# Moving the first norm's inverse root from VectorE to GpSimd in a graph network kernel, with a pipeline one slot shorter and a new end

## The reference

```python
h = x @ W_loop.T ;  g = h @ Wg_loop.T
vals = (h + b_loop) * sigmoid(g + bg_loop)
x1 = layernorm(x + relu((adj.T == 1) @ vals))        # first norm, eps 1e-5
msg = (adj == 1) @ x1
out = layernorm(x1 + msg @ weight[0] + bias)         # second norm
```

## Time and profile before

| | us |
|---|---|
| median of 3 runs | 167.06 (166.71 to 167.41) |
| profiled execution: its own time | 167.7 |
| profiled execution: span from first to last instruction | 166.0 |
| PE busy | 153.1 (92%) |
| DVE busy | 145.5 (88%) |
| ACT busy | 126.2 (76%) |
| POOL busy | 79.9 (48%) |
| message copy on ACT, L534, mean of 31 | 0.580 |
| first norm on ACT for one graph, L582, one instruction | 0.483 |
| second norm on ACT for one graph, L551, mean of 112 | 0.392 |
| memset of one column on POOL, L964 | 0.098 |

### The profile page before, as it was taken

One profiled execution on the slowest core, in us unless ns is written; L12 is line 12 of the kernel. 1 busy time (PEld: TensorE's weight loads), 2 busy tenths in 40 slices (PEclk: granted clock), 3 DMA queues, 4 the chain that ended last, 5 costly groups with the idle time before them and its releaser, 6 DMA issues.

```text
span 166.0 us, 3902 instructions
## 1 busy us (share of the span) xinstructions
PE 153.1 (92%) x1068; PEld 141.9 (85%) x1068; DVE 145.5 (88%) x583; ACT 126.2 (76%) x287; POOL 79.9 (48%) x194
## 2 busy tenths in 40 slices
PE   6499899999999999999999999999999999998910
PEld 2278789999999999999999999999999999997910
DVE  1425999999999999999999999999999999999770
ACT  3318767679988888888888888899888887754670
POOL 4070456264737474747466464646374544446000
PEclk9999999999999999999999999999999999999996
DMA  4999999989598979798998979797979261131133
GB/s 123 332 300 315 396 399 396 391 281 321 153 300 288 380 222 348 275 310 308 285 348 245 374 224 381 211 371 206 370 243 360 31 226 39 41 117 63 67 124 139
DMA packets 18857, 42.76 MB, mean 258 GB/s; under 512 B 2112, under 2 KB 2368, under 8 KB 18832
## 3 DMA queue, kind: packets, MB, share of 16 engines
q1 hardware_dynamic: 13968, 25.24, 42.3%
q0 software_dynamic: 4720, 17.11, 33.8%
q10 hardware_dynamic: 144, 0.13, 0.2%
HBM read 34.08 MB, written 8.39 MB: 256 GB/s over the span
## 4 chain that ended last, share of the span: by engine, by line
PE 85%; DVE 5%; issue 3%; DMA 3%; ACT 1%; ACTq 0%; DVEq 0%; POOLq 0%
PE hg_ps L381 33%; PE msg_ps L411 16%; PE loop_ps L393 15%; PE y_ps L432 15%; DMA gate_b<-gate_bias_dram 3%; PE hg_ps L432 2%; PE hg_ps L428 2%; DVE s_sb L735 1%; ACT gate L524 1%; PE y_ps L428 1%; PE hg_ps L411 1%; ACT out_sb L551 1%; DVE stats L742 0%; DVE hg_ps L638 0%; DVE z_sb L753 0%
## 5 line engine op out<-in xcount | busy, mean ns | idle before, releaser
L381 PE MATMUL hg_ps<-w_all,xt_sb 128*128 128x256 f32 x256 | 63.3, 393 | 2.2 <-DVE w_all L641 2.2
L333 POOL TENSOR_SCALAR x<-s_sb,rstd,nmr 128x128 f32<-128x128 f32 x125 | 55.0, 452 | 3.5 <-issue 0.2
L381 PEld LDWEIGHTS hg_ps<-w_all,xt_sb 128*128 128x128 f32 x256 | 48.2, 198 | 8.9 <-DVE w_all L641 3.1
L515 ACT ACTIVATE hg_ps<-gate_b 128x1024 f32<-128x1024 f32 (+1 forms) x32 | 32.0, 1002 | 9.6 <-DVE vals L727 6.0
L551 ACT ACTIVATE out_sb<-z_sb,rstd 128x128 f32<-128x128 f32 x112 | 38.0, 392 | 0.3 <-DVE rstd L691 0.2
L325 POOL TENSOR_TENSOR nmr<-mean_neg,rstd 128x4 f32<-128x4 f32 x31 | 6.2, 201 | 63.6 <-DVE rstd L691 63.6
L393 PEld LDWEIGHTS loop_ps<-vals,adj_sb 128*128 128x128 f32 x256 | 33.3, 192 | 2.7 <-issue 1.3
L393 PE MATMUL loop_ps<-vals,adj_sb 128*128 128x128 f32 x256 | 33.9, 275 | 0.5 <-DVE s_sb L735 0.5
L411 PE MATMUL msg_ps<-adjt_sb,x 128*128 128x128 f32 x248 | 33.0, 276 | 0.0
L524 ACT ACTIVATE gate<-hg_ps 128x512 f32<-128x512 f32 x32 | 19.1, 596 | 17.0 <-PE hg_ps L381 16.8
L432 PE MATMUL y_ps<-w,msg_t 128*128 128x128 f32 x232 | 30.7, 275 | 0.0
(11 more groups left out here) (66 smaller groups left out, 103.8 us busy)
## 6 DMA issues: line engine op xcount, KB each, us to landing
xt_sb<-x_t_dram SPq DMA_DIRECT2D x32, 256.0 KB, 6.3
x_sb<-x_dram SPq DMA_DIRECT2D x32, 256.0 KB, 6.4
adj_sb<-adj_dram POOLq DMA_DIRECT2D x16, 512.0 KB, 4.5
adjt_sb<-adj_t_dram POOLq DMA_DIRECT2D x16, 512.0 KB, 6.7
out<-out_sb SPq DMA_DIRECT2D x32, 256.0 KB, 3.9
const_sb<-consts_dram POOLq DMA_DIRECT2D x1, 192.0 KB, 5.0
w_all<-w_loop_both_dram ACTq DMA_DIRECT2D x1, 128.0 KB, 2.3
gate_b<-gate_bias_dram POOLq DMA_DIRECT2D x1, 128.0 KB, 4.9
```

What stands on the lines that cost most here:

```text
L333: last = nc.gpsimd.tensor_scalar(x1[:, q % X1_RING, batch(b)], s_sb[:, q % S_RING, batch(b)], r[:, b:b + 1], n[:, b:b + 1], ALU.mult, ALU.add)
L381: last = nc.tensor.matmul(hg_ps[:, q % 2, b, :], xt_sb[:, q % XT_RING, batch(b)], w_gate, start=False, stop=True, skip_group_check=True)
L515: nc.scalar.activation(hg_ps[:, q % 2, 0:graphs, :], gate_b[:, None, :].broadcast_to([P, graphs, 2 * P]), ACT.Copy).then_inc(seeded, 1)
```

## The change

Five things change.

1. DVE no longer computes the first norm's inverse root. It computes var + eps and the negated mean of four columns (`first_moments`) behind the first norm's statistics. POOL raises the variance to the power -0.5 with one elementwise instruction against a constant tile `power`, waits for it, multiplies, and writes x1 as before.
2. The lags become LOOP 1, NORM1 1, MSG 2, Y 3, Z 4, STAT2 5, NORM2 6 (before 1, 2, 3, 4, 5, 6, 7).
3. DVE's nine-step chain serves the second norm alone, 4 columns wide, with one step behind each large instruction.
4. POOL issues the load of `adj` in odd slots and that of `adj_t` in even slots, where it issued both in odd slots.
5. The end is new: `LAST` is 27; only groups 29 and 30 (`INJECTED`) get x1 by the identity matmul, groups 28 and 31 by a DVE add; norm1 of groups 30 and 31 (`SHARED`) is split between ACT and POOL or ACT and DVE; the last chains serve the groups 27 to 29 and 30 to 31; POOL does the second norm of group 27 and of a quarter of group 31; the store of group 30 is issued by ACT.

```diff
-LOOP_LAG, NORM1_LAG, MSG_LAG, Y_LAG, Z_LAG, STAT2_LAG, NORM2_LAG = 1, 2, 3, 4, 5, 6, 7
-LAST = GROUPS - 4
+LOOP_LAG, NORM1_LAG, MSG_LAG, Y_LAG, Z_LAG, STAT2_LAG, NORM2_LAG = 1, 1, 2, 3, 4, 5, 6
+LAST = GROUPS - 5
+CHAIN_A, CHAIN_B = (LAST, LAST + 1, LAST + 2), (LAST + 3, LAST + 4)
+INJECTED = (LAST + 2, LAST + 3)
+SHARED = (GROUPS - 2, GROUPS - 1)
...
             def norm1(q):
                 if exists(q):
-                    t = q + NORM1_LAG
-                    pool.wait_ge(chain_done[t % 2], chain_end(t))
-                    r, n = rstd[:, t % RSTD_RING, 0, :], nmr[:, t % 2, :]
+                    r, n = rstd1[:, q % 2, :], nmr[:, q % 2, :]
+                    pool.wait_ge(mean_done, 2 * q + 2)
+
+                    nc.gpsimd.tensor_tensor(r, var1[:, q % 2, :], power[:, :], ALU.pow).then_inc(rstd1_done, 1)
+                    pool.wait_ge(rstd1_done, q + 1)
+                    nc.gpsimd.tensor_tensor(n, mean_neg[:, q % 2, :], r, ALU.mult).then_inc(nmr_done, 1)
...
+            nc.gpsimd.memset(power[:, :], -0.5).then_inc(power_ready, 1)
             pool.dma_start(gate_b[:, :], gate_bias).then_inc(bias_in, 16)
...
                 norm1(t - NORM1_LAG)
                 if t % 2 == 1:
                     load_adj(t // 2 + 3)
+                else:
                     load_adjt(t // 2 + 2)
...
             loop_sum(GROUPS - 1)
-            message_weights(GROUPS - 4)
-            messages(GROUPS - 3)
+            inject(GROUPS - 3)
             message_weights(GROUPS - 3)
             messages(GROUPS - 2)
+            inject(GROUPS - 2)
+            messages(GROUPS - 1)
             message_weights(GROUPS - 2)
...
-            messages(GROUPS - 1)
             message_weights(GROUPS - 1)
...
-            copy_messages(GROUPS - 4)
-            norm2(GROUPS - 7, every)
             copy_messages(GROUPS - 3)
-            norm2(GROUPS - 6, every)
+            norm2(LAST - 1, every)
+            shared_norm1(GROUPS - 2)
+            shared_norm1(GROUPS - 1)
             copy_messages(GROUPS - 2)
...
+            norm2(LAST + 3, every)
+            act.wait_ge(out_done, LAST + 3)
+            act.dma_start(out[LAST + 3], out_sb[:, (LAST + 3) % OUT_RING, :])\
+                .then_inc(out_st[(LAST + 3) % OUT_RING], 16)
...
+            def first_moments(q):
+
+                m = stats[:, q % STATS_RING, 0:2, :].rearrange("p c (i k) -> p (c i) k", k=3)
+                dve.wait_ge(bn1_done, q + 1)
+
+                await_count(dve, nmr_done, q - 1)
+                ts(var1[:, q % 2, :], m[:, :, 2], 1.0 / P, EPS, ALU.mult, ALU.add).then_inc(mean_done, 1)
+                yield
+                ts(mean_neg[:, q % 2, :], m[:, :, 1], -1.0, None, ALU.mult).then_inc(mean_done, 1)
...
+            last_second_sum(LAST + 1)
+            first_sum(GROUPS - 1)
+            first_stats(GROUPS - 1, 0)
+            first_stats(GROUPS - 1, 1)
+            odd_steps = find_odd()
+            next(odd_steps)
+            for _ in first_moments(GROUPS - 1):
+                pass
+            next(odd_steps, None)
+            last_second_stats(LAST + 1, 0)
+            last_second_stats(LAST + 1, 1)
+            last_second_stats(LAST + 2, 0)
+            last_second_stats(LAST + 2, 1)
+            last_norm1(GROUPS - 1)
+            for _ in last_chain(0, CHAIN_A):
                 pass
+            last_second_stats(LAST + 3, 0)
+            last_second_stats(LAST + 3, 1)
             dve.wait_ge(odd_count, 1)
             nc.vector.tensor_copy(flag[:, :], aux_ps[0:1, 2 * P:2 * P + 1]).then_inc(flag_ready, 1)
+            last_second_sum(LAST + 4)
+            last_second_stats(LAST + 4, 0)
+            last_second_stats(LAST + 4, 1)
+            for _ in last_chain(1, CHAIN_B):
                 pass
+            last_norm2(LAST + 4, (0, 1, 2))
```

More of the change, by code:

```diff
@@ L336, in norm1 @@
-                    last.then_inc(x1_done, 1)
+                        await_count(pool, msg_done, q - X1_RING + 1)
+                        await_count(pool, z_done, q - X1_RING + 1)
+                        for b in range(2 if q in SHARED else GB):
+                            done = nc.gpsimd.tensor_scalar(
+                                x1[:, q % X1_RING, batch(b)], s_sb[:, q % S_RING, batch(b)],
+                                r[:, b:b + 1], n[:, b:b + 1], ALU.mult, ALU.add)
+                        done.then_inc(x1_done, 1)
@@ L413, in messages, with inject @@
                     last.then_inc(msg_done, 1)
+            def inject(q):
+                pe.wait_ge(consts_in, 16)
+                await_x1(q)
+                pe.wait_ge(vals_done, GROUPS - 1)
+                for b in range(GB):
+                    nc.tensor.matmul(y_of(q)[:, batch(b)], ident, x1[:, q % X1_RING, batch(b)],
+                                     start=b == 0, stop=False, skip_group_check=True)
             def message_weights(q):
@@ L420, in message_weights @@
                     if q in y_place:
-                        pe.wait_ge(vals_done, GROUPS)
+                        pe.wait_ge(vals_done, GROUPS - 1 if q < GROUPS - 1 else GROUPS)
                     else:
                         await_count(pe, z_done, q)
[L424 to L429, removed]
                     pe.wait_ge(msgt_done, q + 1)
@@ new lines, in chain, with last_chain @@
+                    yield from inverse_root(m2, rstd2[:, t % RSTD_RING, :], chain_done[t % 2], before,
+                                            tiny[:, t % 2, :, :])
+            def last_chain(k, groups):
+                dve.wait_ge(last_bn, groups[-1] - LAST)
+                if groups[0] == LAST:
+                    dve.wait_ge(bn2_done, LAST + 1)
+                first, end = groups[0] - LAST, groups[-1] - LAST + 1
+                columns = slice(GB * first, GB * end)
+                m2 = last_stats[:, 2 * first:2 * end, :].rearrange("p c (i k) -> p (c i) k", k=3)[:, :, 2]
+                yield from inverse_root(m2, last_rstd[:, columns], last_done[k], 0, last_tiny[:, :, columns])
@@ L806, in _ @@
             message_weight()
-            for t in range(GROUPS + 1):
+            for t in range(GROUPS):
                 steps = chain(t)
-                def step(n):
-                    for _ in range(n):
-                        next(steps, None)
                 if exists(t - Z_LAG):
                     second_sum(t - Z_LAG)
-                    step(1)
+                    next(steps, None)
                     second_stats(t - Z_LAG, 0)
-                    step(1)
+                    next(steps, None)
@@ L831, in _ @@
                     first_stats(t - LOOP_LAG, 1)
-                step(CHAIN_OPS)
+                    next(steps, None)
+                    moments = first_moments(t - LOOP_LAG)
+                    next(moments)
+                    next(steps, None)
+                    next(moments, None)
+                    next(steps, None)
                 if t == 1:
                     message_weight_end()
-            for _ in chain(LAST_CHAIN):
-                pass
+            last_second_sum(LAST + 1)
```

240 lines of the change are left out of this document (118 added, 122 removed).

## The result

The changed kernel takes 178.13 us (median of 4 runs, 176.88 to 180.34) against 167.24 us for the kernel before on the same chip (166.71 to 168.09): ratio 1.067, 95% interval 1.061 to 1.072. It is slower by 11 us, where 165.9 was forecast and 172.5 was the upper end. The profiled execution has a span of 175.2 us and an own time of 176.88, which makes it the fastest of the four.

The account below looks back on a forecast made before the run. PE, busy throughout 26 slots of 4.41 us, was taken as the bound. With p = .30, +.05 + 2.59 + p - 4.43 + .72 - .34 = -1.11 us, so 165.9 us from the median 167.06; range 165.0 to 172.5.

Parts of the forecast that it names:

- the price of the power: POOL's power on four columns, never seen in the trace: taken as .30 us, between .20 and 1.82.
- p: The length of POOL's power in us, on the way from the first norm's statistics to x1.
- Rival 1: Message weight load: PE waits for x1 in every slot, 13 (p-.30) - 1.41 + p, slower from p = .44; chance 37%.
- 8.50 + p: The least time of two slots, in us, if messages wait for x1 because the power is too long.
- the edge: The longest power that stays hidden in a slot: p about .30 us.
- the sum: All terms against the profiled execution: -1.41 + p, plus 13 (p-.30) above .30; -1.11 us for p = .30.
- the fill: Start of the pipeline up to slot 5: PE waits for group 0's x1, costing 2.59 + p us.
- the store: One of the two last stores goes through ACT's queue, so one issue is no longer in line: -.34 us.
- The end: Last projection to last weights: 11.65 us where it took 16.08 before, a gain of 4.43.
- The sum of group 31 on VectorE: Between the last weights and the last norm2, the DVE add of group 31 comes on top: +.72 us.
- The cover for moments on VectorE: DVE's spare time before the gate in each slot, with the added moments: .25 us.
- rival 3: Both moments on DVE take .31 us while norm1 runs on POOL: 3.9 us more, 169.8 us; chance 3%.

Follow-up runs that it names:

- experiment 5: The kernel before with powers of 1, 2, 4, 8, 16 columns and products of 4 and 16 added at GpSimd's end: .199 us shortest, 2.898 longest.
- experiment 1: The changed kernel with the power replaced by a product of the same shape on GpSimd: 167.15 us, ratio 1.001.
- experiment 2: The changed kernel with the power issued twice for each group, the first into a spare tile: 197.17 us, ratio 1.182.
- experiment 10: The changed kernel with the fourth graph of each first norm up to group 29 done by ScalarE instead of GpSimd: 170.59 us, ratio 1.027.
- experiment 11: The kernel before with eight output buffers in place of four: 167.31 us, ratio 1.000.
- experiment 12: The kernel before with sixteen GpSimd tensor_scalar instructions of 128x128 added behind its last adjacency load; the total isn't read.
- experiment 4: The changed kernel with the store of group 30 issued by SyncE behind that of group 31, not by ScalarE: 178.64 us, ratio 1.071.
- experiment 8: The changed kernel with messages, y, z and both steps of the second norm one slot later: 167.63 us, ratio 1.003.
- experiment 9: The changed kernel with messages and later steps one slot later and only group 31's first norm split over three engines: 166.15 us, ratio .9959.
- experiment 7: The changed kernel with x1 as (s - mean) x root in one instruction and the fourth graph's norm1 on VectorE: 179.66 us, ratio 1.076.
- experiment 6: The changed kernel with x1 as (s - mean) x root in one instruction, without product or negated mean: 192.74 us, ratio 1.151.

## Why the prediction was wrong, step by step

**The step that failed is the price of the power.** The prediction took p = .30 between bounds of .20 and 1.82, "by the row of the same engine and shape plus half for arithmetic beyond one product". It is 1.033 (L342, mean of 32). The bounds held it; the choice between them was wrong. For a power the nearer row would have been the other one, the nine dependent steps for the same function. Of "with four columns, the product's .20 is nearly all fixed cost", the premise holds, since a product of 16 columns takes .22. What was made of it, that "four columns of heavier arithmetic needn't double it", is refuted by experiment 5: a power of one column already takes .57, and each column more costs .155. The estimate from the Trainium skill (GPSIMD Engine Reference, section 7, Performance pitfalls for Q7 kernels) of .32 had nine operations put in by me. Its price per column would be .03 us, and .155 was measured, so its 4 cycles per operation can't stand for a power counted in this way.

**The structure of the slot was right.** Rival 1 named the place (the weight load of the messages), the sign of it (PE waits for POOL's multiply-adds) and the bound of 8.50 + p for two slots: with p = 1.03 that is 9.53, and the slots take 4.73 and 4.80. Against 2 x 4.41 it puts the edge at p = .32 rather than the .30 of the sum, and 13 x .71 = 9.2 us above the edge; experiments 1, 2 and 10 confirm the slope with no power, two, and a shortened way: 114.58, 137.27 and 118.54 us against 123.77. The chance of 37% for rival 1 was spread over 167.9 to 187; the range stopped at p = .76.

**That the whole sum fits is luck.** With p = 1.03 it gives -1.41 + 1.03 + 13 x .73 = +9.1 us, and the profiled span grew by 9.2. But the fill came out 1.2 below its forecast for that p, by an early slot 2, the 26 slots .4 below, and the stretches behind the last projection 1.7 above theirs. The medians grew by 10.9.

**A second term failed too.** With the price right, there would have been no gain either: experiment 1, at p = .19, should have gained 1.2 us by the sum and gained nothing (ratio 1.001). The fill and the store, below, are what it lacks.

**The fill** was forecast as 2.59 + p = 3.62 for the true p, and the table shows 2.50. That it looks better is chance ahead of slot 2: it began at 14.76 in the execution before (13.44 to 14.88 in experiments 5, 11 and 12 on that kernel) and at 11.21 in this one. From slot 2 to slot 5 it is 17.74 against 11.69, +6.0. Of the 2.4 us beyond the forecast, 1.6 go with the projection that ran at half speed behind the wait of 3.21: experiment 4's profile, without it, has 16.12. Of the other .8, .4 is slot 4, which took 4.85 us in experiment 4 because x1 is late there already, while the sum charged that from slot 5 on. The last .4 lies ahead of the messages of group 0, as in experiment 1, which with p = .19 is .5 above its own forecast (+3.30 for 2.78).

**The end**: last projection to last weights was forecast as 11.65; experiment 1 has 11.62, the changed kernel 12.19, so the power's length costs .6 there. The sum of group 31 on VectorE was forecast as +.72 and measured at +.76. **The store**: forecast -.34, measured +.76 behind the last norm2. The issue did come earlier: its end lies 1.53 us behind the start of the last norm2, against 1.98 before. But from there to the span's end it is 4.23 us for 3.02. It isn't the queue that the store goes through (experiment 4), nor the number of buffers (experiment 11). What it is stays open; some .7 to .8 is in experiments 1, 8 and 9 too, so it belongs to the new end. These 1.1 us and the .5 of the fill are why the change without the power's cost is no gain either.

**The cover for moments on VectorE** held, and **the shared port** (rival 3) didn't come true: in the changed kernel and in experiment 1 the moments take .17 and .16, and experiment 1 has slots of 4.41 us. The prediction's reading of the earlier trace rows, .151 "alone" and .311 "when norm1 runs on POOL", was too simple. In the whole trace before, L668 starts .6 behind the start of a norm1 27 times; it takes .31 in 16 of these and .15 in the other 11. In the 7 cases with no norm1 beside it, it takes .15 to .17. So the long form comes only beside norm1, but not always there.

## What to carry to other kernels

When work is moved nearer to its user, first write down the slack that is left. Here it was .1 us over a plain product, and an operation that the trace had never shown was put into it. Such a price decides everything and should be measured alone before the order is built on it. If the slack may be too small, keep the distance: the same power behind one slot more costs nothing (experiments 8 and 9), because it then only fills an idle engine. And a way that spans two slots bounds their sum, so a us in it costs half as many us as there are slots, and a cut of it gives back no more.

## What the runs showed of the hardware

- GpSimd's power takes about .41 us + .155 per column of 128 lanes (fitted to experiment 5), 1.03 at 128x4; its product at 128x4 takes .20.
- GpSimd's tensor_scalar over 128x128 takes .45 us for multiply then add and .79 for subtract then multiply, with packed or spaced scalars. VectorE does the latter in .34 (experiment 7).
- Behind a wait of 3.21 us in the fill TensorE ran the next projection in 3.31 us for 1.89, with a granted clock of .50 from 19 to 22 us, which is 1.2 GHz. The same fall is in the profiles of experiment 2 (wait 3.69, projection 3.62) and experiment 6 (wait 3.82, projection 3.25). In experiments 10, 7 and 4, with waits of 2.73, 3.08 and 3.12 us, the projection took 1.89. That is one execution of each, in which other things differ too, so it isn't shown that the wait's length decides.
- A small VectorE tensor_scalar (L668, 128x8) takes .15 to .17 us with no GpSimd norm1 beside it; beside one it takes .31 in 16 of 27 cases and .15 in 11.
